# Cross-attention on one core: the sums of a pair of heads inverted as 16 rows of 64 and spread back through DRAM

## What is computed

```python
x = x + _L0_xattn_ref(_layernorm(x), ctx_2048, ctx_2048)

def _L0_xattn_ref(q, k, v):            # b=4, d=512, m=n=512, 8 heads of 64 rows
    qh = q.reshape(b * h, d // h, m)
    kh = k.reshape(b * h, d // h, -1)
    vh = v.reshape(b * h, c // h, -1)
    qk = jnp.einsum('bdm,bdn->bmn', qh, kh) * scale
    sm = jax.nn.softmax(qk, axis=-1)
    ret = jnp.einsum('bmn,bcn->bcm', sm, vh)
    return ret.reshape(b, c, m)
```

## Time and profile before

| | us |
|---|---|
| median of 3 runs | 1005.21 |
| lowest and highest | 1001.98, 1009.65 |
| the profiled execution | 1008.72 |
| its span in the trace | 1006.9 |
| PE, DVE, ACT, POOL busy in it | 854.4, 732.5, 488.1, 387.3 |

### The profile page before, as it was taken

How to read it: one execution, slowest core, us unless ns; L and a number is a source line. 1 busy time by engine, 2 the same in 40 slices (tenths; PEclk the granted TensorE clock), 3 DMA queues, 4 the chain that set the end, 5 groups by cost and what they waited for, 6 DMA issues and landing times. The chain is left out here.

```text
span 1006.9 us, 15847 instructions
## 1 busy us (share of the span) xinstructions
PE 854.4 (85%) x5106; PEld 438.9 (44%) x5106; DVE 732.5 (73%) x2030; ACT 488.1 (48%) x823; POOL 387.3 (38%) x304
## 2 busy tenths in 40 slices
PE   3998288867998999999688489999999669999997
PEld 2887033323444443444366344344334235454553
DVE  6553478756787887777167579999998369888884
ACT  2665035534565665556422255544454136556664
POOL 2555297969100000000012255666666523333331
PEclk9999569979999999999899869999999979999999
DMA  7885443444122222221369835565554111111100
GB/s 274 317 283 212 134 132 126 138 135 128 50 59 60 66 55 58 61 59 40 108 209 321 303 113 149 168 168 158 164 161 126 50 45 42 43 45 62 43 32 32
DMA packets 92883, 124.06 MB, mean 123 GB/s; under 512 B 43009, under 2 KB 54913, under 8 KB 89729
## 3 DMA queue, kind: packets, MB, share of 16 engines
q1 hardware_dynamic: 67264, 93.68, 29.7%
q10 hardware_dynamic: 23808, 16.78, 5.8%
q0 software_dynamic: 1728, 12.58, 4.0%
HBM read 89.65 MB, written 33.03 MB: 122 GB/s over the span
## 5 line engine op out<-in xcount | busy, mean ns | idle before, releaser
L576 DVE CUSTOM_DVE_ANT_0 b_junk<-b_p,mask_qk 128x128 bf16<-128x128 f32 (+3 forms) x512 | 235.8, 497 | 99.7 <-PE b_p L632 98.1
L536 ACT ACTIVATE b_probs<-b_p 128x512 f32<-128x512 f32 (+1 forms) x352 | 185.5, 558 | 167.9 <-PE b_p L656 167.3
L632 PE MATMUL b_p<-b_ks,b_qs 96*128 96x128 bf16 (+3 forms) x512 | 162.6, 324 | 60.3 <-DMA b_ks<-k_parts 47.8
L654 PE MATMUL b_p<-b_qs,b_ks 98*128 98x512 bf16 (+1 forms) x352 | 132.5, 378 | 2.3
L632 PEld LDWEIGHTS b_p<-b_ks,b_qs 96*128 96x128 bf16 x512 | 51.2, 101 | 171.8 <-DVE b_mx L576 74.3
L1003 ACT ACTIVATE d_probs<-d_p 128x512 f32<-128x512 f32 x128 | 74.4, 594 | 106.4 <-PE d_p L1109 106.1
L762 POOL TENSOR_SCALAR c_veps<-c_mv 128x1 f32<-128x1 f32 x16 | 6.9, 431 | 297.7 <-DVE c_mv L811 297.7
L671 PE MATMUL b_pv<-b_probs,b_vs 128*32 128x192 f32 (+3 forms) x1280 | 106.8, 410 | 0.0
L1027 DVE TENSOR_REDUCE d_mx<-d_p 128x1 f32<-128x512 f32 x128 | 83.8, 671 | 20.1 <-PE d_p L1092 19.2
L976 POOL TENSOR_TENSOR d_halves<-d_probs 128x1024 f32<-128x1024 f32 x32 | 76.3, 2385 | 53.6 <-ACT d_probs L1003 53.5
L656 PE MATMUL b_p<-mask_kq,identb 128*128 128x128 bf16 (+2 forms) x352 | 88.0, 250 | 0.0
(11 more groups left out here) (148 smaller groups left out, 1624.6 us busy)
## 6 DMA issues: line engine op xcount, KB each, us to landing
k<-in_ctx SPq DMA_DIRECT2D x64, 128.0 KB, 2.7
qh<-x_normed_high SPq DMA_DIRECT2D x64, 128.0 KB, 2.8
q_parts<-a_parts SPq DMA_DIRECT2D x16, 384.0 KB, 4.1
b_qs<-q_parts SPq DMA_DIRECT2D x32, 192.0 KB
a_x<-in_x SPq DMA_DIRECT2D x4, 1024.0 KB, 5.8
a_wst<-in_w_gate SPq DMA_DIRECT2D x4, 1024.0 KB, 7.0
a_wst<-in_w_up SPq DMA_DIRECT2D x4, 1024.0 KB, 8.6
a_wst<-in_w_down SPq DMA_DIRECT2D x4, 1024.0 KB, 8.6
```

The costliest lines, as they stand in the source:

```text
L536: nc.scalar.activation(pblock(s2 % 2, kb)[:, j0:j0 + nj, :], p2[(len(EXPS) * s2 + n) % BANKS][:, 0:nj * w].rearrange("p (j c) -> p j c", j ...
L576: nc.vector.tensor_tensor_reduce(out=junk[:, block % UNROLL, 0:w], in0=p1_bank(u, k)[:, 0:w], in1=keep["mask_qk"][:, SEQ - w:], scale=1.0, ...
L632: nc.tensor.matmul(p1_bank(u, k)[:, 0:w], qs[0:STACK, u, j, qt * P:(qt + 1) * P], ks[0:STACK, u, 0:w], start=True, stop=True).then_inc(p1_ ...
L654: nc.tensor.matmul(bank, ks[0:STACK + 2, s2, kb * P:(kb + 1) * P], qs[0:STACK + 2, s2, j0:j0 + nj, kb * P:], start=True, stop=False)
```

## The change

The sums are no longer inverted where they lie. ACT copies `pd` to `den` in the weighing body, behind its first exponential, and behind its second issues two DMAs that lay out one row of each head as 8 rows of 64 in `few`. DVE inverts `few`, 16 rows of 64, in one instruction behind `maximum(2)` of that body. SP stores the result to DRAM (`scr["inv"]`), and, after the loads of `vt` and x1 and the store of x2, waits for that store and issues two loads that spread each head's 512 numbers over 64 partitions of `rden`. DVE's y now waits for these, and stands behind `maximum(2)` of the summing body. PE's next `sum_probs` waits for ACT's copy instead of for the reciprocals. In the feed-forward several semaphores are merged into two, with waits on counts in their place; its instructions and their order stay. The lines of the diff that matter:

```diff
@@ sync
                     sp.dma_start(ql[H:H + 1, s, :].bitcast(F32), mrow[:, s, :].bitcast(F32)).then_inc(m_in[s], 16)
+                if u % 2 and live(first_pair(q, u) - 1, PAIRS):
+                    pr, s = first_pair(q, u) - 1, (u // 2 + 1) % 2
+                    sp.wait_ge(inv_done, pr + 1)
+                    sp.dma_start(scr["inv"][2 * RUNS * pr:2 * RUNS * (pr + 1), :], inv[:, s, :]).then_inc(inv_out, 16)
                 if u % 2 and live(first_pair(q, u), PAIRS):
...
                     sp.dma_start(scr["x2"][bass.ds(P * pr, P), :], x2[:, u // 2, :]).then_inc(x2_out[u // 2], 16)
+                if u % 2 and live(first_pair(q, u) - 1, PAIRS):
+                    pr, s = first_pair(q, u) - 1, (u // 2 + 1) % 2
+                    sp.wait_ge(inv_out, 16 * (pr + 1))
+                    if due(pr - 1):
+                        sp.wait_ge(y_done, pr - 1)
+                    for a in range(2):
+                        at = RUNS * (2 * pr + a)
+                        sp.dma_start(rden[a * H:(a + 1) * H, s, :], scr["inv"][at:at + RUNS, :].rearrange("r c -> (r c)")
+                                     .unsqueeze(0).broadcast_to([H, DIM])).then_inc(rden_in, 16)
@@ scalar
                 exponential(0)
+                pr, s = last_pair(q, u) if u % 2 == 0 else -1, (u // 2 + 1) % 2
+                if live(pr, PAIRS):
+                    act.wait_ge(summed, pr + 1)
+                    if due(32 * pr):
+                        act.wait_ge(few_in, 32 * pr)
+                    nc.scalar.activation(den[:, s, :], pd[:], ACT.Copy).then_inc(den_kept, 1)
...
                 exponential(1)
+                if live(pr, PAIRS):
+                    act.wait_ge(den_kept, pr + 1)
+                    if due(pr - 1):
+                        act.wait_ge(inv_done, pr - 1)
+                    for a in range(2):
+                        act.dma_start(few[a * RUNS:(a + 1) * RUNS, s, :],
+                                      den[a * H:a * H + 1, s, :].rearrange("o (r c) -> o r c", r=RUNS)).then_inc(few_in, 16)
@@ vector
-                def invert(pr, s, part):
+                def invert(pr, s):
                     if live(pr, PAIRS):
-                        at = slice(part * P, (part + 1) * P)
-                        dve.wait_ge(summed, pr + 1)
-                        if part == 0 and due(pr - 1):
-                            dve.wait_ge(y_done, pr - 1)
-                        nc.vector.reciprocal(rden[:, s, at], pd[:, at]).then_inc(rden_done, 1)
+                        dve.wait_ge(few_in, 32 * (pr + 1))
+                        if due(pr - 1):
+                            dve.wait_ge(inv_out, 16 * (pr - 1))
+                        nc.vector.reciprocal(inv[:, s, :], few[:, s, :]).then_inc(inv_done, 1)
...
                 if u % 2:
                     pr, s = first_pair(q, u) - 1, (u // 2 + 1) % 2
-                    invert(pr, s, 3)
                     maximum(1)
                     low_part_of_k()
+                    maximum(2)
                     if live(pr, PAIRS):
-                        dve.wait_ge(rden_done, KD * (pr + 1))
+                        dve.wait_ge(rden_in, 32 * (pr + 1))
                         dve.wait_ge(weighted, pr + 1)
...
                         nc.vector.tensor_tensor(y[:, s, :], pn[:], rden[:, s, :], ALU.mult).then_inc(y_done, 1)
-                    maximum(2)
                     maximum(3)
                 else:
-                    pr, s = last_pair(q, u), (u // 2 + 1) % 2
-                    for part in range(KD - 1):
-                        invert(pr, s, part)
-                        maximum(part + 1)
-                        if part == 0:
-                            low_part_of_k()
+                    maximum(1)
+                    low_part_of_k()
+                    maximum(2)
+                    invert(last_pair(q, u), (u // 2 + 1) % 2)
+                    maximum(3)
@@ tensor
-                    if due(KD * pr):
-                        pe.wait_ge(rden_done, KD * pr)
+                    if due(pr):
+                        pe.wait_ge(den_kept, pr)
```

More of the change, by code:

```diff
@@ L857, in cross_attention @@
     H = XROWS
+    RUNS = DIM // H
     SCALE = float(XROWS) ** -0.5
@@ L870, in cross_attention @@
         mx = m.sb("mx", [P, 2, KD]); mrow = m.sb("mrow", [KD, UNROLL, P], F32R)
+        den = m.sb("den", [P, 2, DIM]); few = m.sb("few", [2 * RUNS, 2, H]); inv = m.sb("inv", [2 * RUNS, 2, H])
         rden = m.sb("rden", [P, 2, DIM]); y = m.sb("y", [P, 2, DIM]); x1 = m.sb("x1", [P, 2, DIM]); x2 = m.sb("x2", [P, 2, DIM])
@@ L880, in cross_attention @@
         scores, exps, halved, totalled, summed, weighted = (m.sem(s) for s in ("scores", "exps", "halved", "totalled", "summed", "weighted"))
-        rden_done, y_done, x2_done = m.sem("rden_done"), m.sem("y_done"), m.sem("x2_done")
+        den_kept, few_in, inv_done, rden_in = m.sem("den_kept"), m.sem("few_in"), m.sem("inv_done"), m.sem("rden_in")
+        inv_out = m.sem("inv_out")
+        y_done, x2_done = m.sem("y_done"), m.sem("x2_done")
         block = ctx.enter_context(nc.Block())
@@ L1175, in feed_forward @@
         y_out = m.sems("y_out")
-        names = ("veps", "ix", "ih", "stat", "aggr", "rstd", "normed", "amax", "sx", "factors", "xr", "xq", "xturned", "xt", "gate", "up", "silu",
-                 "prod", "hpart", "hmax", "htrue", "sh", "fh", "cd", "hr", "hq", "hturned", "ht", "down", "y")
+        names = ("veps", "ix", "ih", "stat", "aggr", "rstd", "xscale", "factors", "xr", "xq", "xturned", "xt", "gate", "up", "silu",
+                 "prod", "hpart", "hscale", "fh", "cd", "hr", "hq", "hturned", "ht", "down", "y")
         S = {n: m.sem(n + "_ok") for n in names}
@@ L1305, in body @@
                         dve.wait_ge(S["xq"], i1 - 1)
[L1306 to L1309, removed]
+                    nc.vector.tensor_scalar(xn[:, s, :], x[:, s1, :], mv[:, s, 0:1], rstd[:, c], ALU.subtract, ALU.mult).then_inc(S["xscale"], 1)
+                    dve.wait_ge(S["xscale"], 3 * i1 + 1)
+                    nc.vector.tensor_reduce(amax[:, c], xn[:, s, :], AX.X, ALU.max, apply_absolute_value=True).then_inc(S["xscale"], 1)
+                    dve.wait_ge(S["xscale"], 3 * i1 + 2)
                     if due(i1 - 1):
                         dve.wait_ge(S["xr"], i1 - 1)
-                    nc.vector.tensor_scalar(sx[:, c], amax[:, c], 1.0 / 127.0, Q_EPS, ALU.mult, ALU.add).then_inc(S["sx"], 1)
-                    dve.wait_ge(S["sx"], i1 + 1)
+                    nc.vector.tensor_scalar(sx[:, c], amax[:, c], 1.0 / 127.0, Q_EPS, ALU.mult, ALU.add).then_inc(S["xscale"], 1)
+                    dve.wait_ge(S["xscale"], 3 * i1 + 3)
                     nc.vector.reciprocal(ix[:, c], sx[:, c]).then_inc(S["ix"], 1)
@@ L1340, in body @@
                     dve.wait_ge(S["hpart"], NB * (j + 1))
[L1341 to L1348, removed]
+                    nc.vector.tensor_reduce(hmax[:, c], hpart[:, s, :], AX.X, ALU.max).then_inc(S["hscale"], 1)
+                    dve.wait_ge(S["hscale"], 4 * j + 1)
+                    nc.vector.tensor_scalar(htrue[:, c], hmax[:, c], cu[:, c], 1.0 / 127.0, ALU.mult, ALU.mult).then_inc(S["hscale"], 1)
+                    dve.wait_ge(S["hscale"], 4 * j + 2)
+                    nc.vector.tensor_scalar(sh[:, c], htrue[:, c], Q_EPS, None, ALU.add).then_inc(S["hscale"], 1)
+                    dve.wait_ge(S["hscale"], 4 * j + 3)
+                    nc.vector.reciprocal(ih[:, c], sh[:, c]).then_inc(S["hscale"], 1)
+                    dve.wait_ge(S["hscale"], 4 * j + 4)
                     if due(2 * (j - 1)):
@@ L1421, in decoder @@
         "xl": nc.dram_tensor("x1_normed_low", (TOKENS, DIM), F32).ap(),
+        "inv": nc.dram_tensor("inverse_sums", (BATCH * XHEADS * DIM // XROWS, XROWS), F32).ap(),
         "x2": nc.dram_tensor("x2", (TOKENS, DIM), F32).ap(),
```

## The result

The kernel with the change takes 1054.29 us in the median of 4 runs (1045.47 to 1059.49), the kernel before beside it 1005.05: a ratio of 1.048, with a 95% interval of 1.039 to 1.056. It is slower by 49 us; 1067 was forecast, in a range from 1030 to 1086. The profiled execution took 1051.86, with a span of 1050.0.

A forecast was written before the change was run, and what follows sets the result against it. PE and POOL were taken to set a floor of 12.3 us a pair, with SP's fixed order deciding after the change. Fourteen loops add 55.6 and the stage's end 6.3, 61.9 in all: 1067 us, range 1030 to 1086.

The forecast's parts named there:

- What bounds the kernel: Cross-attention pair: PE and POOL set a floor of 12.3 us; PE can use only 0.65 of DVE's 3.2 gained.
- The SP queue decides: SP's list waits for the inversion, delaying the row of maxima: loop 15.5 us, not 13.03 (S: weighing body's first second scores).
- y: DVE's scaling in the summing body waits for `rden` until S + 12.0; covered by SP's queue, otherwise a pair of 13.4.
- The clock: PE's pause of about 3 us per pair brings a half-speed stretch, adding 1.5 us: loop 17.0.
- The sum: Fourteen cross-attention loops of 17.0 instead of 13.03 add 55.6 us; with 6.3 at the end, 61.9.
- End of the stage: Last cross-attention pair cannot hide its DMA chain: 4.8 us later, 6.3 with one more slow stretch.
- Nothing: The feed-forward's merged semaphores and PE's wait for ACT's copy cost no time.
- the clock holds: Rival: same SP queue, but pauses inside the dense stage do not lower the clock; 1045 us, chance 0.23.
- Short DMAs: Rival: `few` lands in 1.7 us, SP issues take 0.35 to 0.5, loop 14.5; 1030 us, chance 0.09.
- Long DMAs: Rival: 3.3 us into `few` and out to DRAM, 0.6 per issue, loop 19.0 with slow clock; 1096 us, chance 0.09.
- the queue catches up: Rival: held SP queue issues the row of maxima by S + 9.8, pair 12.3; 1000 us, not slower, chance 0.09.

The follow-up runs named there:

- e1: Kernel after, with SP storing the previous pair's inverse so it waits for no fresh inversion (y wrongly scaled); ratio 1.007 to the kernel before.
- e2: Kernel before, with one added wait in SP's list with vt, for DVE's third reciprocal; no DMA added; ratio 1.022 to the kernel before.
- e5: Kernel after, SP's list reordered: q of the next body and its row of maxima moved up, k last; ratio 1.015 to the kernel before.
- e3: Kernel after, with twelve unread matmuls added behind each pair's sum to fill PE's pause; ratio 1.041 to the kernel before.
- e6: Kernel after with SP's order put right, and y moved behind `maximum(3)`; ratio 1.011 to the kernel before.
- e9: Kernel before, with POOL's first addition split into two instructions, the first behind the second exponential; ratio 0.990 to the kernel before.
- e4: Kernel after, SP's list reordered: inversion and store waits last, behind vt, x1, x2 and the next body's q loads; ratio 1.052 to the kernel before.

## Why the prediction was right, and where it was off

*What bounds the kernel.* Right in kind: PE could use little of the time that DVE gained. The floor was put at 12.3 a pair and was 12.77 in e1. The step that failed is the one that POOL's total "does not depend on DVE": it grew from 1.29 to 1.74 when DVE's subtraction started ahead of it, and 0.45 is just what is missing.

*The SP queue decides.* Right, and shown three times: by the hold put into the kernel before (e2), by taking the fresh result away (e1) and by the order (e5). The sum had L937 at S + 13.0 and a loop of 15.5 with a clock that holds; e3 gives 15.5 at clock 1.00. Its parts were less exact than their sum, and that they cancel is luck: with the slow clock the row was to leave at S + 14.5 and left at 13.9, and what came behind it took so much longer. ACT's two issues took 0.64 each, not 0.37, and DVE could start on `few` 2.35 after the first of them, where 2.75 were counted. The store of the inverse was issued in 0.33, not 0.55, and landed in 1.3. The load of q low took 3.2 from 672.79 to PE's start, not 2.7, and decides ahead of the row of maxima. SP stood 4.8 us a pair for the inversion, where some 4 were forecast.

*y.* `rden` needed 3.8 to land where I had 2.7, the wait ahead of y was 2.3 a pair, and it was covered, as forecast; e6 shows what it costs uncovered. The 13.4 given for a pair without that cover does not follow from its own terms: `maximum(3)` at 13.4 is needed at S' + 0.5, so 12.9; e5 has 12.9 to 14.4.

*The clock.* Right in kind and in size: 1.5 was taken, 1.6 to 2.0 measured (17.1 against 15.5 in e3, 15.1 and 15.3 in the two loops at full clock). Over the ten slow loops the clock is 0.90 in the mean; "below 0.9 in the slices" holds for about half of the page's slices. What I had not seen is that the slow stretch can begin with the work itself (659.1) and not 1 to 1.6 us behind its start as in the rows I had.

*The sum.* The forecast of 1067 was 13 too high, and 8.9 of that are this term, which was mis-sized. Fourteen loops of 17.0 were counted, 55.6 us. From the first L1136 of a weighing body at 594.89 to the same at 823.97 are 229.08 us, against 182.42: 46.7. Of the fourteen only ten, from 625.30 to 796.54, took 17.1. The first two ran at a clock of 1.00 and 0.99 and took 15.1 and 15.3. The last two took 15.4 and 12.0, when SP had no k and then no q left to load; I had asked whether the row of maxima still passes through the loop, and not what else still stands in the queue.

```profile
609.98:625.30 15.32, 12.09 (x48) 5.27 (x46) 8.35 (x14) 7.00 (x13) 9.25 (x6) 0.99 0.55 156
625.30:796.54 171.24, 135.26 (x461) 56.43 (x460) 84.47 (x140) 69.98 (x130) 89.79 (x51) 0.90 0.49 140
796.54:811.93 15.39, 13.14 (x47) 5.49 (x46) 8.45 (x14) 7.00 (x13) 7.45 (x5) 0.92 0.39 121
811.93:823.97 12.04, 10.69 (x42) 4.14 (x41) 3.77 (x7) 5.03 (x9) 7.67 (x5) 1.00 0.33 90
```

*End of the stage.* 4.8, or 6.3 with a slow stretch, were counted; y comes 21.1 after S (823.97 to 845.10) against 16.5: 4.6. The two together, 51.3, are what the stage lost. *Nothing*, for the merged semaphores, was right: 199.6 and 199.7 behind the stage.

*The rivals.* That the clock holds is refuted by the trace (0.51 behind the pause shown) and by e3. Its support had a slip: "pauses of up to 0.9" between 603 and 785 leaves out the stop of 1.33 ahead of 784.62. Short DMAs: `few` took 2.35 and not 1.7, and its issues 0.64. Long DMAs: only `rden`, with 3.8, was beyond its 3.3. That the queue catches up is refuted too: the twelve issues from 666.62 to 673.43 are 6.8 us of a pair of 17, and e5 wins 42 us by nothing but their order. The Trainium skill (DMA: Bandwidth & Descriptors, Issuing engines are not separate DMA queues) says that the time to initiate a DMA is usually small relative to the DMA itself. Here issues of 0.33 to 0.63 stand beside landings of 1.3 to 3.8, and behind a wait they add up.

## What to carry to other kernels

A queue that issues in a fixed order is on the path of everything behind a wait that is put into it. When a step becomes a chain of DMAs, look up what else stands behind each of its waits, and put the loads that the next body needs ahead of it, after reading what those loads wait for themselves. And a gain on an engine is worth what the others wait for it, here 0.66 us a pair of the 3.2 gained; the better place to look was the chain after the last exponential, where e9 gained 10.6 in the stage.

## What the runs showed of the hardware

- A pause of PE does not by its length alone tell whether the clock falls. One of 2.27 us ahead of 609.64 in the kernel after was followed by a loop at 0.99. Of two of 2.12 in e2, the one ahead of 687.65 was followed by a stretch at the half level (0.50 from 690 to 692), the one ahead of 717.62 by none. In e5 the clock was 0.50 from 757 to 759, and PE's longest stops in the ten us ahead of that were 0.99 and 0.69, at 754.97 and 756.38.
- DVE's subtraction with two inputs in SBUF and POOL's addition, 0.69 and 1.28 us alone, cost about half a microsecond more when they start close together, and the one that starts second pays: 1.74 for POOL's behind DVE's start (e1), 1.24 for DVE's 0.6 behind POOL's (before).
- A load that spreads 2 KB over 64 partitions took 3.8 us to land in the kernel after and 2.9 in e4; the 4 KB store that it reads landed in 1.3 and 2.2. Why they differ with the order was not tried.
